# The attention output's projection by two matrix products per row block instead of three

## The reference

```python
xn = _layernorm(x, axis=-1)                      # x is 2 x 4096 x 512
# attention on a compressed latent (64 wide)
c = (xn @ W_to_kv.T) @ W_compress.T
ch = layernorm(c) * ln_gamma + ln_beta
q, k, v = ch @ W_q.T, ch @ W_k.T, ch @ W_v.T     # each 64 wide, rotary on q and k
attn = softmax(causal(q k^T / 8))                # per batch, 4096 x 4096
o = attn @ v
z = o @ W_comp2lat.T
out = z @ W_to_kv + z @ W_out_res.T + b_out_res
# routed experts: 16, two per token, and a shared expert
ffn = shared(xn) + sum over 2 experts of weight * expert(xn)
return x + out + ffn
```

## Time and profile before

| | |
|---|---|
| median of 3 runs | 1821.04 us (1817.68 to 1822.61) |
| the profiled execution | 1825.91 us, span 1824.1 us |
| PE busy | 1745.7 us, 96% |
| DVE busy | 1175.5 us, 64% |
| ACT busy | 751.7 us, 41% |
| POOL busy | 663.7 us, 36% |

### The profile page before, as it was taken

The page is one execution under the profiler, slowest core; times in us unless marked ns, Lnnn a source line. Parts: engine busy times, 40 slices in busy tenths (PEclk is TensorE's granted clock), DMA queues, the critical chain, the costliest instruction groups (busy, mean ns, idle before and its releaser), DMA issues. The chain is left out here.

```text
span 1824.1 us, 28057 instructions
## 1 busy us (share of the span) xinstructions
PE 1745.7 (96%) x8413; PEld 1392.8 (76%) x8413; DVE 1175.5 (64%) x2284; ACT 751.7 (41%) x1295; POOL 663.7 (36%) x676
## 2 busy tenths in 40 slices
PE   5699999999999998999999999999999989999998
PEld 3587777787777886788788777778888867777776
DVE  7777777777766763455555555555555447788786
ACT  3232332333222322333333334333333357777875
POOL 2544544445454442333434333343433320111110
PEclk9799999999999999999999999999999999999999
DMA  7767777766777666644544546555445438899896
GB/s 249 245 196 238 231 228 216 243 193 193 229 223 215 199 181 187 205 137 154 185 169 165 174 166 200 174 180 179 158 166 177 168 66 178 198 247 217 209 220 173
DMA packets 149934, 352.52 MB, mean 193 GB/s; under 512 B 20476, under 2 KB 41916, under 8 KB 149824
## 3 DMA queue, kind: packets, MB, share of 16 engines
q1 hardware_dynamic: 97276, 234.52, 39.8%
q0 software_dynamic: 43968, 104.91, 22.4%
q10 hardware_dynamic: 8580, 11.64, 2.4%
HBM read 208.24 MB, written 146.70 MB: 195 GB/s over the span
## 5 line engine op out<-in xcount | busy, mean ns | idle before, releaser
L1487 POOL DMA_INDIRECT expert_rows<-res,ids_all x143 | 149.8, 1048 | 445.8 <-ACT res L1309 436.9
L1428 DVE TENSOR_REDUCE mx<-emb 128x1 f32<-128x512 f32 (+3 forms) x288 | 175.0, 641 | 107.3 <-PE emb L1228 74.4
L70 PE MATMUL egu<-w,rT_0h 128*128 x576 | 186.5, 405 | 0.8 <-issue 0.8
L70 PE MATMUL egu<-w,rT_1h 128*128 x568 | 182.6, 402 | 0.0
L1405 DVE TENSOR_TENSOR eh<-egu,esg 128x256 f32<-128x256 f32 x143 | 60.6, 424 | 182.6 <-ACT esg L1299 170.7
L1683 ACT ACTIVATE ex<-sc 128x1024 f32<-128x1024 f32 (+4 forms) x176 | 144.2, 820 | 67.8 <-PE sc L1630 49.6
L1035 POOL DMA_INDIRECT token_list<-tok,slot x128 | 127.4, 995 | 116.7 <-DVE slot L741 80.8
L1482 POOL DMA_INDIRECT rows<-xn_scratch,rows_all x137 | 132.5, 967 | 49.5 <-issue 43.1
L1299 ACT ACTIVATE esg<-egu 128x256 f32<-128x256 f32 x143 | 54.9, 384 | 203.4 <-PE egu L70 173.1
L1756 POOL DMA_DIRECT2D base<-expert_rows x32 | 42.1, 1560 | 261.1 <-DMA base<-base_scratch 241.5
L1629 PE MATMUL sc<-qh,khl 128*128 128x512 f32 (+3 forms) x288 | 111.9, 389 | 11.4 <-ACT pr_1h L1683 3.5
(11 more groups left out here) (286 smaller groups left out, 4548.9 us busy)
## 6 DMA issues: line engine op xcount, KB each, us to landing
w<-expert_parts SPq DMA_DIRECT2D x64, 768.0 KB
base<-expert_rows POOLq DMA_DIRECT2D x32, 1024.0 KB, 13.6
expert_parts<-ew_h SPq DMA_DIRECT2D x32, 768.0 KB
expert_parts<-ew_l SPq DMA_DIRECT2D x32, 768.0 KB
x<-x SPq DMA_DIRECT2D x16, 1024.0 KB
xn_scratch<-xn SPq DMA_DIRECT2D x16, 1024.0 KB, 8.6
base_scratch<-xb SPq DMA_DIRECT2D x16, 1024.0 KB
base<-base_scratch SPq DMA_DIRECT2D x16, 1024.0 KB, 6.3
```

Source lines behind the costliest of these rows:

```text
L70: mm = pe.matmul(dst, w, m, start=(first and i == 0), stop=(last and i == len(terms) - 1))
L1428: dve.tensor_reduce(mx[n % 2][:, j, c:c + 1], mb[g % 2][:, 0:width], AX.X, ALU.max).then_inc(m_red, 1)
L1487: pool.indirect_dma_start(parts_d[:, :], bass.IndirectOffsetOnAxis(ap=ids_all[:, t:t + 1], axis=0), res[t % 2][:, :], None, bounds_check=2 ...
```

## The change

The low part of rows 64 to 127 of `ob`, and the product of rows 64 to 127 with the low weights, are no longer made. The two tiles of a group now hold:

- high tile: as before, both halves rounded, to be multiplied by `mo_h`, the high weights in both halves;
- the other tile: in partitions 0 to 63 a copy of the high part of the first half, in partitions 64 to 127 the low part of the first half. Its weights `mo_l` hold the low part in partitions 0 to 63 and the high part in 64 to 127.

So two products per block do high by high, high by low and low by high for the first half, and high by high for the second.

```diff
-        wz, wo, mo, mo2 = ka[0][:, :], ka[1][:, :], qa[0][0:C, :], qa[1][:, :]
+        wz, wo, mo, mo2 = ka[0][:, :], ka[1][:, :], qa[0][0:C, :], qa[1][0:C, :]
...
-                    act.copy(mo2, mb[1][:, :])
+                    act.copy(mo2, mb[1][0:C, :])
+                    act.copy(mop[1][C:P, :], mb[1][0:C, :])
                     act.copy(mop[0][:, :], mb[1][:, :]).then_inc(mo_ev, 1)
...
-                dve.tensor_tensor(mop[1][:, :], mo2, value(mop[0][:, :]), ALU.subtract).then_inc(mo_ev, 1)
+                dve.tensor_tensor(mop[1][0:C, :], mo2, value(mop[0][0:C, :]), ALU.subtract).then_inc(mo_ev, 1)
...
-                        mm = pe.matmul(ob[k % 2][:, 2 * i:2 * i + 2], oT[k % 2][0][:, i * P:(i + 1) * P], last[:, :], start=True, stop=True)
+                        mm = pe.matmul(ob[k % 2][:, 2 * i:2 * i + 2], oT[k % 2][1][:, i * P:(i + 1) * P], last[:, :], start=True, stop=True)
...
-                parts(pe, pj[j % 2][:, :], [([a[:, j * P:(j + 1) * P] for a in oT[k % 2]], [a[:, :] for a in mop])]).then_inc(p_done, 1)
+                for a in range(2):
+                    mm = pe.matmul(pj[j % 2][:, :], oT[k % 2][a][:, j * P:(j + 1) * P], mop[a][:, :], start=a == 0, stop=a == 1)
+                mm.then_inc(p_done, 1)
...
-                dve.tensor_tensor(oT[k % 2][1][:, :], ob[k % 2][:, :], value(oT[k % 2][0][:, :]), ALU.subtract).then_inc(o_low, 1)
-                dve.wait_ge(o_low, k + 1)
-                dve.tensor_tensor(oT[k % 2][0][C + ONE:C + ONE + 1, :], ob[k % 2][ONE:ONE + 1, :], value(oT[k % 2][0][ONE:ONE + 1, :]),
-                                  ALU.subtract).then_inc(o_ev, 1)
+                high, rest = oT[k % 2]
+                dve.tensor_copy(rest[0:C, :], value(high[0:C, :]))
+                dve.tensor_tensor(rest[C:P, :], ob[k % 2][0:C, :], value(high[0:C, :]), ALU.subtract).then_inc(o_ev, 1)
```

More of the change, by code:

```diff
@@ L1535, in attend @@
         s_done, e_done, pv_done, low_done = sem("s_done"), sem("e_done"), sem("pv_done"), sem("low_done")
-        o_hi, o_low, o_ev = sem("o_hi"), sem("o_low"), sem("o_ev")
+        o_hi, o_ev = sem("o_hi"), sem("o_ev")
         l_done, l_ev, p_done, p_ev = sem("al_done"), sem("l_ev"), sem("p_done"), sem("p_ev")
```

## The result

| | before | after |
|---|---|---|
| median of 6 runs each | 1820.29 us (1817.68 to 1822.61) | 1810.76 us (1807.55 to 1812.12) |
| ratio of the runs | | 0.9942, 95% interval 0.9930 to 0.9953 |
| profiled execution's span | 1824.1 us | 1808.4 us |
| first score product to end of span | 333.36 us | 323.85 us |

The medians differ by 9.5 us, and the ratio makes 10.6 us of it, with 8.6 to 12.7 us as its interval. The forecast was 1809.3 us, 11.7 us less.

A forecast was written before the change was run, and what follows sets the result against it. PE, 97% busy in `attend`, was taken as the bound, with transfers next. Terms -14.7 + 2.5 + 1.0 - 0.5 = -11.7 us took the median from 1821.04 to 1809.3 us; range 1806 to 1813, 8 in 10 1804 to 1817.

The forecast's parts named there:

- the ring: Buffers of `base` in `attend`: position 13's combine would wait for transfers, costing PE 0 to 2.1 us, taken as 1.0.
- The product's price on PE, 0.23 us: PE in `attend`: each product removed gives back 0.23 us, 64 of them 14.7 us, the main term.
- What the waits take back: PE's waits for ACT's exponentials in `attend`: savings lost at 14 waits, at most 3.2 us, taken as 2.5.
- PE's shown waits for ACT: Sign in the changed profile, where projections run: these waits would rise from 6.1 to some 8.5 us.
- DVE has 20% left, so outside the end it counts as nothing: DVE at each of 16 groups' ends: gains 0 to 0.34 us, counted as nothing except after the last group.
- The end: After the last group: DVE's 0.34 us in full and products at the lower clock, 0 to 1.0 us gained, taken as 0.5.
- The folded weights: Before `attend`: one more ACT copy of about 0.59 us, hidden in ACT's idle time, 0; uncovered, 0.6 us once.
- the transfers as a bound: Rival in `attend`: the DMA share can reach only 0.95, giving 1814 us, a gain between 3 and 8 us; chance 0.17.
- The rival on the slower side: DVE's new copies delay POOL's issues, late combines idle PE and its clock falls in `attend`: 1839 us; chance 0.03.

The follow-up runs named there:

- the old tiles: Kernel before with two of its three products per block, its tiles and DVE subtractions kept: ratio 0.9951 to before, stretch between first and last reciprocal 277.11 us.
- Shortening ACT alone: ACT's rounded exponential of two-block steps over half the columns: kernel before 0.9927, stretch 273.94 us; changed kernel 0.9882, 262.57 us.
- shortening both: ACT's rounded exponential and DVE's low part of two-block steps over half the columns: kernel before 0.9929, stretch 271.87 us; changed kernel 0.9860, 260.66 us.
- shortened alone: Changed kernel with only DVE's low parts of two-block steps over half the columns: ratio 0.9929 to before, stretch 270.89 us.
- with three products: Changed kernel with a third product per block put back, its tiles and DVE work kept: ratio 0.9992 to before, stretch 283.33 us.
- the run with fewer accumulations: Changed kernel without the first of the two accumulating transfers of each group: ratio 0.9941 to before, stretch 275.34 us.
- less rounding on DVE: Changed kernel with 12 instead of 24 two-block steps rounded by DVE, the others by ACT: ratio 0.9929 to before, stretch 275.67 us.

## Why the prediction was right, and where it was off

The direction, the range and the main mechanism held: 1810.76 us against 1809.3, and 9.5 us gained in the medians against 11.7. PE's products are the gain, and the loop through ACT takes part of it back. But that the number came so near is partly luck. The loop took 3.3 us more than its term, and two errors the other way hid half of that: the ring's 1.0 us never came, and the new tiles gave 0.65 us in the stretch where nothing was counted.

- **The product's price on PE, 0.23 us.** Right. In all kernels the distance from one product of 512 columns to the next was 0.22 to 0.23 us wherever nothing delayed it. The 436 ns of the table of groups would have been wrong by a factor of two. The 131 ns for a sustained stream that the Trainium skill gives on the page "TensorE: Matmul & The Clock Gate", section "Back-to-back issue gap", and that the prediction weighed, was not seen here either.
- **"What the waits take back": 2.5 us, at most 3.2.** This is the term that was mis-sized. The stretch lost 13.8 - 7.98 = 5.8 us, or 6.9 with the old tiles. The reasoning in the earlier trace rows was right, that a saving made while ACT is busy without a pause is lost. The step that failed is counting the places from PE's idle time in the earlier trace rows: the products' shown durations hide delays under 0.17 us and shorten every other one. In the same window the weight loads' waits show 24 places, not 14; at 0.23 us each, 24 places make 5.5 us, which is about what was lost. That match was found afterwards, and I have not tested it as a rule. That the loss stands in front of the score products is shown by the start-to-start delays, 13.2 us before and 18.5 in the changed kernel. PE's shown waits for ACT, forecast at 8.5 us, came to 9.0, so this check alone would have passed the term.
- **ACT alone.** I laid the waits to ACT. Shortening ACT alone brought back 2.7 us, shortening both 2.6 us as measured and 4.4 us with the ring's stop added back. DVE's low parts are a part of the loop that I had left out: shortened alone they gave the changed kernel 4.5 us.
- **"DVE has 20% left, so outside the end it counts as nothing": 0.** It counted 0.65 us with three products and 1.76 with two, of which 0.3 us belong to the end and the rest is small for traces of one execution. But DVE was late in places with a fifth of its time free: ACT waited 9.7 us for its low parts.
- **The ring, 1.0 us.** Nothing came of it at position 13, where the store of position 10 now stood in front of the accumulations and the load behind it could go after 5.3 instead of 15.4 us. The term had taken this distance as fixed. The fear itself was well placed: the both-shortened kernel stopped at exactly this position, and the combine stood there also with ACT alone (2.5 us) and with the low parts alone (1.1 us) shortened.
- **The end, 0.5 us on top of its products.** From the last ACT operation on `ob` to the end of the span it was 1824.1 - 1813.59 = 10.5 us before and is 1808.4 - 1799.11 = 9.3 us now. Of these 1.2 us, 4 x 0.23 = 0.9 are the products', so 0.3 us are on top. They are DVE's: from the start of that ACT operation to PE's row sums it was 2.09 us and is 1.79. The prediction read the 0.63 us of the first block's third product as the lower clock, and the granted clock was 0.65 from 1816 to 1818 us. In the changed kernel it was 0.95 from 1801 to 1803 us, where the first block's second product is shown as 0.39 us long, and 0.50 from 1803 to 1808 us. All this is from one execution each, and the part behind the last reciprocal, 6.85 us in the changed kernel, was 7.01 to 7.35 us in three kernels with the same end.
- **The folded weights, 0, and the transfers as a bound.** Nothing in the traces speaks against the first; the second is excluded for the changed kernel by the run with fewer accumulations.
- **The new copies and POOL.** Ten of POOL's issues of a pair still took 2.57 us and two took 2.60. The longest, 2.90 us at 1765.24, had one of the old rounding copies beside it. Of the new copies two overlapped an issue, and there it was the copy that took longer, 0.58 and 0.66 instead of 0.41 us. The rival on the slower side had no support.

In sum, with what the runs showed: in the stretch 13.8 us of products, less 5.8 us taken back, plus 0.65 us from DVE make 8.6 us; behind the stretch come 0.9 us; together 9.5 us. The 5.8 us are themselves the rest of this sum; what supports them on their own are the 5.2 to 5.3 us by which the delays before score products grew.

No complete kernel tried here beats the changed one; the faster ones leave work out. The one with less rounding on DVE was timed at 0.9929 (0.9903 to 0.9955) against 0.9942 (0.9930 to 0.9953), which cannot be told apart, and its stretch is 0.3 us longer.

## What to carry to other kernels

In this kernel PE was busy 97% and fed by a loop through two engines at 80%, and work taken from it was worth less than its price, and less with each further cut: 9.7, 8.0 and 4.7 us of 13.8. To size the loss, look at start-to-start distances or at the waits of the short instructions beside the long ones, since idle time between overlapping instructions hides the short delays. And a transfer that comes too late in one order may come in time in another: ask what is in the queue ahead of it, and not only how long it took.

## What the runs showed of the hardware

- A DVE copy of 64 x 512 f32 to fp32r within SBUF took 0.41 to 0.42 us, and 0.58 and 0.66 us in the two places where it overlapped the issue of a pair of accumulating transfers by POOL, which stayed at 2.57 us. A rounding copy of 128 x 1024 lay beside the issues of 2.86 and 2.90 us.
- A product of 512 columns came 0.23 us behind the one before it in dense stretches at full clock, and is shown as 0.39 to 0.40 us long; at the end, with a granted clock of 0.65 in the window from 1816 to 1818 us, the distances were 0.43 us (1817.19 to 1817.62).
- A DVE subtraction of 64 rows from PSUM that writes to partitions 64 to 127 from inputs in 0 to 63 took 684 ns, just as one that stays in its partitions.
- A 1 MB store at one position landed in time for the next load to be issued after 5.3 us when it was issued 1.3 us ahead of a pair of accumulating transfers, and after 15.4 us when it was issued 2.4 us behind them.
